# A recurrent block with a mixture of experts: first-layer outputs turned and halved by the pair

## The chip, the cores and the metric

One core of a Trainium2 chip runs one launch. The metric is the device time of the launch in microseconds (us).

## What is computed

The input has 4 sequences of 512 tokens with 256 features. It is normalised, and two branches are added to it. The first is a gated linear recurrence with a gated feed-forward layer of 1024 hidden features. The second is a mixture of 8 experts of which each token uses two:

```python
router_logits = x_flat @ w_router
top_vals, top_idx = jax.lax.top_k(router_logits, TOP_K)
probs = jax.nn.softmax(top_vals, axis=-1)
...
h = jnp.einsum('nc,ecd->ned', x_flat, w_fc)
h = jnp.square(jax.nn.relu(h))
y = jnp.einsum('ned,edc->nec', h, w_proj)
out = jnp.einsum('nec,ne->nc', y, w_tok)
...
x = x + _L0_attn_ref(xn, ...) + _L0_ffn_ref(xn, ...)
```

## The kernel before

Products of full precision are made of three products of halves: a tensor is split into a high part (a copy by ScalarE, ACT) and a low part (a subtraction by VectorE, DVE), and TensorE (PE) adds high by high, low by high and high by low.

After the routing, the tokens lie in DRAM sorted by expert, in 39 blocks of 128 rows (`NB`), each of one expert; two neighbouring blocks are a pair (`NP` = 20). A block runs through these helpers, whose names are the same on several engines:

- `load_pair` (SyncE's queue, SP) loads a pair into `xq`; `block_turn` (DVE) transposes it in 32 x 32 squares, `block_in` (ACT, then DVE) makes its halves, by the pair.
- `expert_in` (PE) is the first layer of one block. `block_relu` (ACT) and `block_square` (DVE) work by the pair, `store_act` (ACT's queue) stores the pair to DRAM in two DMAs, and `load_act` (SP) loads it back in four, in another order of rows, into a buffer `aq`. Only the loads wait for the store (`act_stored`), and the next turn of it waits for the loads (`aq_loaded`).
- `act_turn` (DVE, L1389) transposes one block from `aq` into `aT_raw`, `block_middle` makes `aT_hi` (ACT, L959) and `aT_lo` (DVE, L1396). There are two buffers `aT`, used in turn by blocks.
- `expert_out` (PE) is the second layer of a block, into one of two banks. `block_y` (ACT, L969) takes the result with its weight into `yb`, and `scatter` (GpSimd) writes it to DRAM.

The feed-forward layer runs beside this. Its 32 tiles are counted by d. `gate_up(d)` (PE), `gate` (ACT), `up` (DVE), `split_gu` (ACT and DVE) and `down(d)` (PE) follow each other; `take_down` (DVE) adds a finished sequence. Each engine has an order written out by hand. From d = 11 (`FIRST`) to 23 (`LAST`) a tile has two or three block steps; in step i PE does `expert_out(i - 8)` and `expert_in(i)`, parts of `gate_up` and `down` lie between, and DVE begins with `act_turn(i - 7)`. In some tiles a third step holds the output projection (`PROJECT`) or the turning (`TURN`) of a sequence of the first branch. At d = 24 and 25 (`DRAIN`) the last eight blocks' second layers run among the tiles. Only then are the outputs of the experts loaded and added (`add_sum`).

PE waits in `expert_out(i)` for the block's low half (`a_split`) and for `block_y(i - 2)` (`y_ready`). ACT's order at d = 24 is:

```python
split_gu(d - 1); block_relu(NP - 1); block_y(d0 - 1); block_middle(d0 + 1)
store_act(NP - 2); store_act(NP - 1)
block_y(d1 - 1); block_middle(d1 + 1); gate(d)
block_y(d2 - 1); block_middle(d2 + 1); block_y(d3 - 1); block_middle(d3 + 1)
```

Here d0 to d3 are blocks 31 to 34. All buffers lie in one arena at addresses given by hand, and some lie over others that are dead by then.

Of the kernel before, what the change touches and what calls it, by code (L numbers as in the profile page):

```python
# [14 lines left out]
P = 128  # L15
# [21 lines left out]
def recurrent_moe_block(nc, x, pre_norm_w, w_a, w_i, w_v, out_proj_w, decay_bias, ffn_norm_w,  # L37
# [35 lines left out]
    with ExitStack() as ctx:  # L73
# [27 lines left out]
        ident, ones = put("ident", [P, P]), put("ones", [P, P])  # L101
        before, ones_bf = put("before", [P, P], BF16), put("ones_bf", [P, P], BF16)
        one = put("one", [P, 1])
        half, minus_half, minus_one = put("half", [P, T]), put("minus_half", [P, T]), put("minus_one", [P, T])
        lane = put("lane", [P, P])
# [5 lines left out]
        HE = 2 * E  # L111
        Wr_wide = put("Wr_wide", [P, K, (2 * B - 1) * HE], F32R)
        Wr_at = (B - 1) * HE
        stats, mv = put("stats", [P, T, 6]), put("mv", [P, T, 2])
# [4 lines left out]
        of_slot = put("of_slot", [P, 2 * NP, 2])  # L119
# [101 lines left out]
        h2 = [h2_first] + [put(f"h2_{b}", [P, J, D], F32, cum_at if b != 2 else yb_at) for b in range(1, B)]  # L221
        junk = [junk_first] + [put(f"junk{b}", [P, J, D], BF16, cum_at if b != 2 else yb_at) for b in range(1, B)]
# [158 lines left out]
        def _(sp):  # L381
# [75 lines left out]
        def _(pe):  # L457
# [276 lines left out]
            def expert_out(i):  # L734

                if i >= 0:
                    if i == 0:
# [58 lines left out]
        def _(act):  # L796
# [156 lines left out]
            def block_middle(i):  # L953

                if 0 <= i < NB:
                    act.wait_ge(a_turned, i + 1)
                    if i >= 2:
                        act.wait_ge(pj_done, i - 1)
                    A.activation(aT[i % 2][0][:, :, :], aT[i % 2][2][:, :, :], ACT.Copy).then_inc(a_hi, 1)  # L959
# [101 lines left out]
            for d in range(FIRST, B * M):  # L1061
                if d <= LAST:
                    for v, i in enumerate(blocks_of(d)):
# [15 lines left out]
                elif d <= DRAIN:  # L1079
# [30 lines left out]
                if d in PROJECT or d in TURN:  # L1110
                    i = block_after(d)
                    block_y(i - LAG - 1)
                    block_middle(i - LAG + 1)
# [7 lines left out]
                    if d in TURN:  # L1121
                        split_h2(TURN[d], range(1, 2))

        @block.vector
        def _(dve):
# [148 lines left out]
            def experts():  # L1274
                be = [P, NB + 1, E]
                chain.step(V.tensor_tensor(past[:, :, :], blk_end[:, None, :].to_broadcast(be),
                                           lane[:, 0:NB + 1, None].to_broadcast(be), ALU.is_le))
# [103 lines left out]
            def act_turn(i):  # L1381

                if 0 <= i < NB:
                    n, v = divmod(i, 2)
                    u = act_home(n)
                    dve.wait_ge(aq_loaded[u], 16 * (P // Q) * (n // 2 + 1 if u < 2 else 1))
                    if i >= 2:
                        dve.wait_ge(pj_done, i - 1)
                    V.transpose(aT[i % 2][2][:, :, :].rearrange("p k (g s) -> p k g s", s=Q),  # L1389
                                aq[u][:, :, v, :, :]).then_inc(a_turned, 1)  # L1390

            def block_middle(i):

                if 0 <= i < NB:
# [343 lines left out]
```

## Time and profile before

| what | us |
|---|---|
| median of 3 runs | 271.26 (270.78 to 271.38) |
| the profiled execution's own time | 270.97 |
| its span | 269.2 |
| PE busy | 258.8 |
| DVE busy | 213.2 |
| ACT busy | 160.3 |

Times in the rows count from the start of the span. Busy times of PE are modelled from pipelined matmuls, so a busy PE is not PE at its peak. An engine's idle time is put down to what ended it.

### The profile page before, as it was taken

The page shows a single profiled execution, that of the slowest core. Times are in us where ns is not written, and L with a number is a line of the kernel's source. Part 1 is how long each engine was busy: PE and PEld are TensorE (multiplying, and loading weights), DVE is VectorE, ACT ScalarE, POOL GpSimd, SP SyncE. Part 2 cuts the span into 40 slices and gives each one's busy share as a digit, 9 for nine tenths or more (in the row PEclk, how much of TensorE's full clock was granted, in tenths as well). Part 3 has the DMA queues.
Part 4 walks back from the last instruction along what each step waited for, and adds up shares of the span by engine and source line. Part 5 has one row for each costly group of instructions (what it writes and reads, how often), then busy time and mean ns, then how long its engine had stood idle before and what let it go on. Part 6 is the DMA issues. An engine that isn't in the chain of part 4 may idle for free.

```text
span 269.2 us, 5120 instructions
## 1 busy us (share of the span) xinstructions
PE 258.8 (96%) x1593; PEld 227.2 (84%) x1593; DVE 213.2 (79%) x402; ACT 160.3 (60%) x323; POOL 117.1 (43%) x145
## 2 busy tenths in 40 slices
PE   5999999999999999999899999999999999999994
PEld 4767778888888888989798899989999999898883
DVE  4889999999846999699889895778778677732994
ACT  3888889995566554254764565466676665532221
POOL 6499004788878830016133244087336434550000
PEclk9999999999999999999999999999999999999999
DMA  6999962448621224639888777579979977529962
GB/s 198 354 391 323 322 187 99 158 169 254 234 98 49 92 83 93 48 79 181 154 201 191 181 186 172 128 150 223 211 157 235 202 181 176 136 76 299 385 237 78
DMA packets 107077, 49.62 MB, mean 184 GB/s; under 512 B 72006, under 2 KB 103756, under 8 KB 107052
## 3 DMA queue, kind: packets, MB, share of 16 engines
q1 hardware_dynamic: 90352, 32.48, 48.6%
q0 software_dynamic: 5664, 11.44, 14.6%
q10 hardware_dynamic: 11036, 5.38, 6.7%
q8 instruction: 14, 0.23, 0.3%
q14 instruction: 11, 0.09, 0.1%
HBM read 27.32 MB, written 21.96 MB: 183 GB/s over the span
## 4 chain that ended last, share of the span: by engine, by line
PE 69%; DVE 16%; issue 6%; ACT 4%; POOL 2%; DMA 1%; ACTq 0%; DVEq 0%; POOLq 0%
PE ps L459 62%; PE ps L547 5%; DVE rows_x L1331 2%; DVE xgT_raw L1363 2%; DVE act_e L1379 2%; DVE aT_raw L1389 1%; POOL rn L1597 1%; PE ps L560 1%; DMA rows_x<-in_L_attn_x_dram 1%; DVE stats L1134 1%; PE ps L476 1%; ACT aT_hi L959 1%; DVE hT_lo L1162 1%; DVE guT_lo L1301 1%; DVE cum L1188 1%
## 5 line engine op out<-in xcount | busy, mean ns | idle before, releaser
L1661 POOL DMA_INDIRECT y_dram<-yb,home_u x39 | 38.5, 988 | 59.6 <-ACT yb L969 57.2
L1638 POOL DMA_INDIRECT xs_dram<-rows_x,slot_u x32 | 38.6, 1205 | 11.3 <-issue 10.2
L459 PE MATMUL ps<-h2T_lo,Wgu_hi 128*128 128x512 f32 (+1 forms) x132 | 41.8, 386 | 0.0
L459 PE MATMUL ps<-h2T_hi,Wgu_hi 128*128 128x512 f32 (+1 forms) x132 | 41.0, 392 | 0.2 <-DVE rows_x L1202 0.2
L459 PE MATMUL ps<-h2T_hi,Wgu_lo 128*128 128x512 f32 (+1 forms) x132 | 40.4, 387 | 0.0
L459 PE MATMUL ps<-Wd_hi,guT_hi 128*128 128x256 f32 x128 | 36.5, 285 | 1.2 <-DVE guT_lo L1316 0.8
L959 ACT ACTIVATE aT_hi<-aT_raw 128x256 fp32r<-128x256 f32 x39 | 16.3, 417 | 33.9 <-DVE aT_raw L1389 33.8
L459 PE MATMUL ps<-Wd_hi,guT_lo 128*128 128x256 f32 x128 | 36.2, 282 | 0.0
L459 PE MATMUL ps<-Wd_lo,guT_hi 128*128 128x256 f32 x128 | 36.1, 282 | 0.0
L1296 DVE TENSOR_TENSOR gu<-gu,ps 128x512 f32<-128x512 f32 x31 | 21.1, 682 | 15.5 <-PE ps L459 15.3
L903 ACT ACTIVATE gu<-ps 128x512 f32<-128x512 f32 x31 | 18.5, 596 | 23.3 <-PE ps L459 21.7
L1396 DVE TENSOR_TENSOR aT_lo<-aT_raw,aT_hi 128x256 fp32r<-128x256 f32 x39 | 16.5, 424 | 16.7 <-ACT aT_hi L959 16.7
L923 ACT ACTIVATE guT_hi<-gu 128x512 fp32r<-128x512 f32 x31 | 19.4, 627 | 17.1 <-DVE gu L1296 13.9
L459 PEld LDWEIGHTS ps<-h2T_lo,Wgu_hi 128*128 128x128 f32 x132 | 24.5, 188 | 5.1
L459 PEld LDWEIGHTS ps<-h2T_hi,Wgu_lo 128*128 128x128 f32 x132 | 24.5, 188 | 4.8
L459 PEld LDWEIGHTS ps<-Wd_hi,guT_hi 128*128 128x128 f32 x128 | 24.1, 188 | 3.2 <-DVE guT_lo L1316 1.2
L459 PEld LDWEIGHTS ps<-Wd_lo,guT_hi 128*128 128x128 f32 x128 | 24.1, 189 | 1.2
L1301 DVE TENSOR_TENSOR guT_lo<-gu,guT_hi 128x512 fp32r<-128x512 f32 x31 | 20.9, 676 | 4.1 <-ACT guT_hi L923 3.8
L459 PEld LDWEIGHTS ps<-Wd_hi,guT_lo 128*128 128x128 f32 x128 | 24.1, 188 | 0.0
L459 PEld LDWEIGHTS ps<-h2T_hi,Wgu_hi 128*128 128x128 f32 x132 | 21.8, 188 | 2.2 <-DVE rows_x L1202 0.5
L969 ACT ACTIVATE yb<-ps,of_slot 128x256 f32<-128x256 f32 x39 | 18.4, 472 | 6.3 <-issue 3.5
L1613 POOL TENSOR_SCALAR sn<-ssq 128x4 f32<-128x4 f32 x4 | 0.8, 195 | 44.1 <-ACT junk L876 30.6
(174 smaller groups left out, 619.3 us busy)
## 6 DMA issues: line engine op xcount, KB each, us to landing
xs_dram<-blank SPq DMA_DIRECT2D x1, 5160.0 KB, 26.7
xq<-xs_dram SPq DMA_DIRECT2D x80, 64.0 KB
act_dram<-act_e ACTq DMA_DIRECT2D x40, 128.0 KB
aq<-act_dram SPq DMA_DIRECT2D x80, 64.0 KB, 2.4
sums<-y_dram SPq DMA_DIRECT2D x8, 512.0 KB, 7.8
Wgu_raw<-in_L_attn_w_gate_up_dram SPq DMA_DIRECT2D x4, 512.0 KB, 9.1
Wfc_raw<-in_L_ffn_w_fc_dram SPq DMA_DIRECT2D x16, 128.0 KB
Wpj_raw<-in_L_ffn_w_proj_dram SPq DMA_DIRECT2D x4, 512.0 KB, 6.5
```

Source lines behind the costliest of these rows:

```text
L459: return nc.tensor.matmul(dst, lhs, rhs, start=start, stop=stop, skip_group_check=group)
L547: last = nc.tensor.matmul(ps[:, aside(b) + side, (j % 2) * D:(j % 2 + 1) * D], dec[b][:, k, j * P:(j + 1) * P], Wo[:, k, :], start=k == 0, ...
L903: A.activation(gu[d % 2][:, :], ps[:, gu_bank(d), :], ACT.Silu).then_inc(sg_ready, 1)
L923: A.activation(guT[d % 2][0][:, :], gu[d % 2][:, :], ACT.Copy).then_inc(gu_hi, 1)
L959: A.activation(aT[i % 2][0][:, :, :], aT[i % 2][2][:, :, :], ACT.Copy).then_inc(a_hi, 1)
L969: A.activation(yb[i % YB][:, :], ps[:, PJ[i % 2], 0:D], ACT.Copy, scale=of_slot[:, i, 0:1]).then_inc(y_ready, 1)
L1296: V.tensor_tensor(gu[d % 2][:, :], gu[d % 2][:, :], ps[:, gu_bank(d) + 1, :], ALU.mult).then_inc(gu_ready, 1)
L1301: V.tensor_tensor(guT[d % 2][1][:, :], gu[d % 2][:, :], guT[d % 2][0][:, :].bitcast(F32), ALU.subtract).then_inc(gu_split, 1)
L1331: ins = V.tensor_tensor(Y[b][:, :, :], Y[b][:, :, :], sums[u][b][:, :, :], ALU.add)
L1396: V.tensor_tensor(aT[i % 2][1][:, :, :], aT[i % 2][2][:, :, :], aT[i % 2][0][:, :, :].bitcast(F32), ALU.subtract).then_inc(a_split, 1)
L1638: pool.indirect_dma_start(out=xs_dram, in_=rows_x[:, b, j, :], in_offset=None, out_offset=bass.IndirectOffsetOnAxis(ap=slot_u[:, n:n + 1], ...
L1661: pool.indirect_dma_start(out=y_dram, in_=yb[i % YB][:, :], in_offset=None, out_offset=bass.IndirectOffsetOnAxis(ap=home_u[:, i:i + 1], ax ...
```

## The change

The first layer's outputs are turned and halved by the pair: one transposition, one copy and one subtraction of 128 x 512 instead of two each of 128 x 256. The two `aT` buffers hold a pair each and so grow from 1 KB to 2 KB a half. The room for them is that of `yb`, which moves half to a place of its own and half over tables of the routing (`ones`, `before`, `ones_bf`, `Wr_wide`). `of_slot` moves over `stats`, the table `lane` is cut to the columns in use, and the buffer `h2` of sequence 2 comes to lie over the second `aT`; pair 1's turn waits until it has been read. Order and waits change with it: the pair's turn and its high half are at the even step i = 2n + 6 of pair n, the low half at the odd step after it, and the order in the drain is another.

```diff
+        early_at = room(0)
+        ones, before, ones_bf = put("ones", [P, P]), put("before", [P, P], BF16), put("ones_bf", [P, P], BF16)
+        HE = 2 * E
+        Wr_wide = put("Wr_wide", [P, K, (2 * B - 1) * HE], F32R)
+        lane = put("lane", [P, NB + 1])
...
-        aT = [turned_halves(f"aT{u}", 1) for u in range(2)]
-        yb_at = over[0]
-        yb = [small(f"yb{u}", [P, D]) for u in range(YB)]
+        h2_at = over[0] + 4 * KB
+        aT = [turned_halves(f"aT{u}", 2) for u in range(2)]
+        yb_at = room(2 * KB)
+        yb = [put(f"yb{u}", [P, D], F32, (yb_at, early_at)[u // 2] + D * 4 * (u % 2)) for u in range(YB)]
...
 (load_act, SP)
-                    sp.wait_ge(a_turned, 2 * n - 2)
+                    sp.wait_ge(a_turned, n - 1)
...
 (expert_out, PE)
-                    pe.wait_ge(a_split, i + 1)
+                    if v == 0:
+                        pe.wait_ge(a_split, n + 1)
                     if i >= 2:
                         pe.wait_ge(y_ready, i - 1)
-                    layer(PJ[i % 2], 0, aT[i % 2], slice(0, P), Wpj, expert[i], pj_done)
+                    layer(PJ[v], 0, aT[n % 2], slice(v * P, (v + 1) * P), Wpj, expert[i], pj_done)
...
 (ACT)
+            def block_middle(n):
+                if 0 <= n < NP:
+                    act.wait_ge(a_turned, n + 1)
+                    if n >= 2:
+                        act.wait_ge(pj_done, 2 * n - 2)
+                    A.activation(aT[n % 2][0][:, :, :], aT[n % 2][2][:, :, :], ACT.Copy).then_inc(a_hi, 1)
...
-                        block_middle(i - LAG + 1)
                         if i % 2 == 0:
+                            block_middle((i - LAG) // 2 + 1)
                             block_relu(i // 2 - 1)
...
                     if d == LAST + 1:
                         block_relu(NP - 1)
-                    block_y(d0 - 1)
-                    block_middle(d0 + 1)
-                    if d == LAST + 1:
+                        block_y(d0 - 1)
                         store_act(NP - 2)
                         store_act(NP - 1)
-                    block_y(d1 - 1)
-                    block_middle(d1 + 1)
+                        block_middle(NP - 3)
+                    else:
+                        block_middle(NP - 2)
+                        block_y(d0 - 1)
+                        block_middle(NP - 1)
                     gate(d)
-                    block_y(d2 - 1)
-                    block_middle(d2 + 1)
-                    block_y(d3 - 1)
-                    block_middle(d3 + 1)
+                    block_y(d0)
+                    block_y(d1)
+                    block_y(d2)
...
 (DVE)
+            def act_turn(n):
+                if 0 <= n < NP:
+                    u = act_home(n)
+                    dve.wait_ge(aq_loaded[u], 16 * (P // Q) * (n // 2 + 1 if u < 2 else 1))
+                    if n == 1:
+                        dve.wait_ge(h2T_done, K * 3)
+                    if n >= 2:
+                        dve.wait_ge(pj_done, 2 * n - 2)
+                    V.transpose(aT[n % 2][2][:, :, :].rearrange("p k (a s) -> p k a s", s=Q),
+                                aq[u][:, :, :, :, :].rearrange("p k v g c -> p k (v g) c")).then_inc(a_turned, 1)
...
-                        act_turn(i - LAG + 1)
+                        if i % 2 == 0:
+                            act_turn((i - LAG) // 2 + 1)
+                        else:
+                            block_middle((i - LAG + 1) // 2)
                         if v == 0 and d - 1 in PROJECT:
                             add_residual(PROJECT[d - 1], 1)
                         if v == 0:
                             split_gu(d - 1)
-                        block_middle(i - LAG + 1)
...
-                    d0, d1, d2, d3 = drained_by(d)
-                    act_turn(d0 + 1)
                     split_gu(d - 1)
                     if d == LAST + 1:
                         block_square(NP - 1)
-                    block_middle(d0 + 1)
-                    act_turn(d1 + 1)
-                    block_middle(d1 + 1)
-                    act_turn(d2 + 1)
-                    up(d)
-                    block_middle(d2 + 1)
-                    act_turn(d3 + 1)
-                    block_middle(d3 + 1)
+                        block_middle(NP - 4)
+                        act_turn(NP - 3)
+                        up(d)
+                        block_middle(NP - 3)
+                        act_turn(NP - 2)
+                    else:
+                        block_middle(NP - 2)
+                        act_turn(NP - 1)
+                        up(d)
+                        block_middle(NP - 1)
```

## Rows read from the trace of the kernel before

**Rows 1.** The page's engines: busy us (share of the span), instructions.

```profile
PE 258.8 (96%) x1593; PEld 227.2 (84%) x1593; DVE 213.2 (79%) x402; ACT 160.3 (60%) x323; POOL 117.1 (43%) x145
```

**Rows 2.** Three stretches: busy us of PE, weight loads, DVE, ACT, GpSimd; clock, DMA.

```profile
113.00:154.00 41.00, 39.52 (x258) 35.06 (x257) 36.46 (x66) 22.71 (x52) 11.95 (x13) 1.00 0.77 158
154.00:222.00 68.00, 67.83 (x475) 63.45 (x474) 51.37 (x103) 42.24 (x99) 31.74 (x33) 1.00 0.84 186
222.00:238.20 16.20, 16.09 (x108) 14.48 (x107) 10.63 (x23) 9.36 (x23) 7.74 (x8) 1.00 0.59 146
```

**Rows 3.** Groups by line and shape: busy us, mean ns | idle before, releaser.

```profile
L1389 DVE STREAM_TRANSPOSE aT_raw<-aq 128x256 f32<-128x256 f32 x39 | 16.9, 433 | 0.5 <-DMA aq<-act_dram 0.5
L459 PE MATMUL ps<-Wpj_hi,aT_hi 128*128 x78 | 16.7, 295 | 1.4 <-DVE aT_lo L1396 1.2
L1396 DVE TENSOR_TENSOR aT_lo<-aT_raw,aT_hi 128x256 fp32r<-128x256 f32 x39 | 16.5, 424 | 16.7 <-ACT aT_hi L959 16.7
L959 ACT ACTIVATE aT_hi<-aT_raw 128x256 fp32r<-128x256 f32 x39 | 16.3, 417 | 33.9 <-DVE aT_raw L1389 33.8
L1363 DVE STREAM_TRANSPOSE xgT_raw<-xq 128x512 f32<-128x512 f32 x20 | 14.1, 705 | 0.0
L1370 DVE TENSOR_TENSOR xgT_lo<-xgT_raw,xgT_hi 128x512 fp32r<-128x512 f32 x20 | 13.7, 687 | 0.9
L931 ACT ACTIVATE xgT_hi<-xgT_raw 128x512 fp32r<-128x512 f32 x20 | 12.4, 619 | 6.0 <-DVE xgT_raw L1363 6.0
```

**Rows 4.** Groups of the weight loads (PEld), 113 to 240 us.

```profile
L459 PEld LDWEIGHTS ps<-Wpj_hi,aT_hi 128*128 128x128 f32 x78 | 12.7, 188 | 4.4 <-issue 3.3
```

**Rows 5.** The last of the four loads of pair 0, by tile: issue, landing.

```profile
L404 SPq DMA_DIRECT2D aq<-act_dram x1: 488/488/488, 121.7 to 121.7; - x1
...
DMA to landing us min/median/max: 4.0/4.0/4.0
```

**Rows 6.** Timeline, 123 to 129 us: start, us, instruction, idle before and releaser.

```profile
124.06 0.67 DVE L1301 TENSOR_TENSOR guT_lo<-gu,guT_hi 128x512 fp32r<-128x512 f32 x1
...
125.67 0.28 PE L459 MATMUL ps<-Wd_hi,guT_hi 128*128 128x256 f32 x1
...
125.85 1.21 DVE L1291 TENSOR_TENSOR Wpj_lo<-Wpj_raw,Wpj_hi 128x1024 fp32r<-128x1024 f32 x1
...
128.56 0.48 PE L459 MATMUL ps<-Wpj_hi,aT_hi 128*128 x2 [0.57 <-DVE aT_lo L1396]
```

**Rows 7.** Timeline of the drain, 217 to 237 us.

```profile
218.04 0.43 ACTq L950 DMA_DIRECT2D act_dram<-act_e  x1
...
222.06 0.69 DVE L1379 TENSOR_TENSOR act_e<-ps,act_e 128x512 f32<-128x512 f32 x1
...
225.42 0.47 ACT L969 ACTIVATE yb<-ps,of_slot 128x256 f32<-128x256 f32 x1 [1.43 <-issue]
...
226.10 0.59 ACT L903 ACTIVATE gu<-ps 128x512 f32<-128x512 f32 x1
...
226.95 0.39 PE L459 MATMUL ps<-Wpj_hi,aT_hi 128*128 x2
...
227.15 0.45 DVE L1389 STREAM_TRANSPOSE aT_raw<-aq 128x256 f32<-128x256 f32 x1 [0.49 <-DMA aq<-act_dram]
...
229.69 1.28 DVE L1324 TENSOR_TENSOR rows_x<-rows_x,ps 128x512 f32<-128x512 f32 x2
...
230.89 0.44 DVE L1389 STREAM_TRANSPOSE aT_raw<-aq 128x256 f32<-128x256 f32 x1
...
232.37 0.47 PE L459 MATMUL ps<-Wpj_hi,aT_hi 128*128 x2
...
236.72 0.40 PE L459 MATMUL ps<-Wpj_hi,aT_hi 128*128 x2
```

**Rows 8.** The last of the four loads of pair 16, by tile.

```profile
L404 SPq DMA_DIRECT2D aq<-act_dram x1: 493/493/493, 218.6 to 218.6; - x1
...
DMA to landing us min/median/max: 3.5/3.5/3.5
```

More of the change, by code:

```diff
@@ L100, in recurrent_moe_block @@
         PRE_W, FFN_W, BIAS = 0, K, 2 * K
-        ident, ones = put("ident", [P, P]), put("ones", [P, P])
-        before, ones_bf = put("before", [P, P], BF16), put("ones_bf", [P, P], BF16)
+        ident = put("ident", [P, P])
+        early_at = room(0)
[3 more added lines that the diff above has]
+        lane = put("lane", [P, NB + 1])
+        assert top[0] - early_at >= 2 * KB
         one = put("one", [P, 1])
         half, minus_half, minus_one = put("half", [P, T]), put("minus_half", [P, T]), put("minus_one", [P, T])
-        lane = put("lane", [P, P])
         rank8 = put("rank8", [P, E])
@@ L108, in recurrent_moe_block @@
         Wr = put("Wr", [P, K, E])
-        HE = 2 * E
-        Wr_wide = put("Wr_wide", [P, K, (2 * B - 1) * HE], F32R)
         Wr_at = (B - 1) * HE
-        stats, mv = put("stats", [P, T, 6]), put("mv", [P, T, 2])
+        stats_at = room(4 * T * 6)
+        stats, mv = put("stats", [P, T, 6], F32, stats_at), put("mv", [P, T, 2])
         tv, rn1, nb1, negm = put("tv", [P, T]), put("rn1", [P, T]), put("nb1", [P, T]), put("negm", [P, T])
@@ L118, in recurrent_moe_block @@
         slot_u = put("slot_u", [P, TOP * T], U32)
-        of_slot = put("of_slot", [P, 2 * NP, 2])
+        of_slot = put("of_slot", [P, 2 * NP, 2], F32, stats_at)
         no_home, home_u = put("no_home", [P, 2 * NP]), put("home_u", [P, 2 * NP], U32)
@@ L219, in recurrent_moe_block @@
         act_e = [put(f"act_e{u}", [P, 2, D], F32, slot_at[2] + 4 * KB + 2 * D * 4 * u) for u in range(2)]
-        h2 = [h2_first] + [put(f"h2_{b}", [P, J, D], F32, cum_at if b != 2 else yb_at) for b in range(1, B)]
-        junk = [junk_first] + [put(f"junk{b}", [P, J, D], BF16, cum_at if b != 2 else yb_at) for b in range(1, B)]
+        h2 = [h2_first] + [put(f"h2_{b}", [P, J, D], F32, cum_at if b != 2 else h2_at) for b in range(1, B)]
+        junk = [junk_first] + [put(f"junk{b}", [P, J, D], BF16, cum_at if b != 2 else h2_at) for b in range(1, B)]
         ps = ctx.enter_context(nc.psum_tensor("ps", [P, 8, 512], F32))
@@ L736, in expert_out @@
                 if i >= 0:
+                    n, v = divmod(i, 2)
                     if i == 0:
@@ L1122, in _ @@
                         split_h2(TURN[d], range(1, 2))
+                    if i % 2 == 0:
+                        block_middle((i - LAG) // 2 + 1)
         @block.vector
@@ L1276, in experts @@
                 chain.step(V.tensor_tensor(past[:, :, :], blk_end[:, None, :].to_broadcast(be),
-                                           lane[:, 0:NB + 1, None].to_broadcast(be), ALU.is_le))
+                                           lane[:, :, None].to_broadcast(be), ALU.is_le))
                 chain.step(V.tensor_reduce(expert_f[:, :], past[:, :, :], AX.X, ALU.add))
@@ L1379, in block_square, with block_middle @@
                     V.tensor_tensor(mine, ps[:, FC[n % 2], 0:size], mine, ALU.mult).then_inc(act_ready, 1)
-            def act_turn(i):
-                if 0 <= i < NB:
-                    n, v = divmod(i, 2)
+            def act_turn(n):
+                if 0 <= n < NP:
                     u = act_home(n)
                     dve.wait_ge(aq_loaded[u], 16 * (P // Q) * (n // 2 + 1 if u < 2 else 1))
[L1387 to L1394, printed above, removed]
-                    dve.wait_ge(a_hi, i + 1)
-                    V.tensor_tensor(aT[i % 2][1][:, :, :], aT[i % 2][2][:, :, :], aT[i % 2][0][:, :, :].bitcast(F32),
+                    if n == 1:
[4 more added lines that the diff above has]
+                                aq[u][:, :, :, :, :].rearrange("p k v g c -> p k (v g) c")).then_inc(a_turned, 1)
+            def block_middle(n):
+                if 0 <= n < NP:
+                    dve.wait_ge(a_hi, n + 1)
+                    V.tensor_tensor(aT[n % 2][1][:, :, :], aT[n % 2][2][:, :, :], aT[n % 2][0][:, :, :].bitcast(F32),
                                     ALU.subtract).then_inc(a_split, 1)
@@ L1555, in _ @@
                     i = block_after(d)
-                    act_turn(i - LAG + 1)
-                    block_middle(i - LAG + 1)
+                    if i % 2 == 1:
+                        block_middle((i - LAG + 1) // 2)
+                    elif TURN.get(d) != 2:
+                        act_turn((i - LAG) // 2 + 1)
                     if d in PROJECT:
@@ L1570, in _ @@
                         split_h2(TURN[d], range(1, 2))
+                    if TURN.get(d) == 2:
+                        act_turn((i - LAG) // 2 + 1)
             add_down(B - 1)
@@ L1668, in tables @@
                 G.iota(rank8[:, :], pattern=[[-1, E]], base=E, channel_multiplier=0, **I)
-                G.iota(lane[:, :], pattern=[[1, P]], base=0, channel_multiplier=0, **I).then_inc(tables_ready, 1)
+                G.iota(lane[:, :], pattern=[[1, NB + 1]], base=0, channel_multiplier=0, **I).then_inc(tables_ready, 1)
             root_x(1, slice(0, 2))
```

8 lines of the change are left out of this document (1 added, 7 removed).

## The prediction

> **What bounds the kernel now.** I read the page's engine rows first: TensorE (PE) is busy 96% of the span [rows 1]. By stage, between 154 and 222 us PE has 67.83 of 68 us busy and its clock is granted in full in all three stages [rows 2]. So a faster VectorE (DVE) or ScalarE (ACT) gives time back only where PE waited for it. What is touched here is the way of the first layer's outputs into the second layer: turn on DVE, high half on ACT, low half on DVE. The groups by line show that this way stalls those two engines a lot (33.8 us of ACT before `aT_hi`, 16.7 us of DVE before `aT_lo`) and PE very little: 1.2 us before the second layer's first product [rows 3]. Idle time of the weight loads ahead of the same product is the upper view of that: 4.4 us, of which 3.3 without a releaser [rows 4].
>
> Last I read the timeline at the two ends of the block stage, where the order of the engines changes: around the first second-layer product (128.56 us) and in the drain, d = 24 and 25 [rows 6, 7]. The reader is to see there how close a load of `aq` lands to its use.
>
> **The change part by part.**
>
> *Fewer, larger instructions.* 39 turns of 433 ns become 20 of 705; 39 subtractions of 424 become 20 of 687; 39 ACT copies of 417 become 20 of 619 [rows 3]. DVE gives back 16.9 + 16.5 - 20 x (0.705 + 0.687) = 5.6 us, ACT 16.3 - 12.4 = 3.9 us. The round trip DVE, ACT, DVE inside one step also goes, since the low half is now made a step after the turn: the 16.7 us of DVE waits mostly vanish. On PE the worth is what PE waited: at least 1.2 us, at most 3.3 [rows 3, 4]. The first of these waits, 0.57 us at 128.56, stays, because the product there also needs `Wpj_lo`, whose 1.21 us run at 125.85 just ahead [rows 6]. That leaves 0.6 to 2.7; I take the middle, **-1.6 us**.
>
> The Trainium skill bears on this in "VectorE: DVE Perf Modes", section "The TRN2 errata — SBUF-src ops pay a fixed extra latency per instruction": many small tiles pay a fixed cost each, so tiles of 512 elements or more are advised. The rows agree on the size: 705 ns against twice 433 [rows 3]. "Perfetto Trace Analysis", section "Optimizing Scalar/DVE Operations", adds the condition that grouping helps "if the engine is saturated", and DVE at 51.37 of 68 us is not [rows 2]; by the first rule alone the result would be the gain of the first rival below, by the second none.
>
> *Moves of buffers.* `yb`, `stats`/`of_slot` and the tables change places only, and no instruction is added; the one new wait of the reuse (`h2T_done` before pair 1's turn) is at a place where the turn already stands behind the split of h2. `lane` shrinks in one GpSimd instruction that nothing on this path waits for late in the kernel. I cost all of it at nothing, within 0.1 us either way.
>
> *The turn comes a step earlier.* A pair is stored after its square in step 2n+2, and its turn stood at the head of steps 2n+7 and 2n+8; now one turn stands at the head of step 2n+6. Behind it on DVE are `split_gu` or `up`, `block_turn` and `block_square` of the same step; behind the copy it feeds on ACT are `block_relu` and `gate`. So a load that lands late now stops both engines.
>
> At the start: pair 0's last load is issued at 121.7 us and lands 4.0 us later, at 125.7 [rows 5]. DVE starts `guT_lo` at 124.06 and PE uses it at 125.67 [rows 6]. After the change the turn comes first: 125.7 + 0.71 + 0.67 = 127.1, so PE waits 1.4 us. Then `block_turn` 0.71, square 0.65, `Wpj_lo` 1.21 and the pair's subtraction 0.69 give 130.4 for the first second-layer product, against 128.56: **+1.8 us** [rows 3, 6]; the square is taken as that of the drain lasts, 0.69 less its overlap [rows 7]. Were the load early, the same sum from 124.06 is 128.7: +0.1. From here on the -1.6 works back, so PE should come to d = 24 between 1 us early and 1 us late.
>
> *The drain.* This decides. At d = 24 ACT now does the copy of pair 17 first, then `gate(24)`, and only then `block_y(31)`; PE's block 33 waits for that `y`. Before, `y` of block 31 ran at 225.42, ahead of all this. Pair 17's turn waited for its load until 227.15, the one turn of the kernel that did [rows 3, 7]. After: 227.15 + turn 0.71 + copy 0.62 + gate 0.59 + y 0.47, less small overlaps (`gate` starts before its forerunner's end), is 229.45; PE did block 33 at 226.95 [rows 3, 7]. So **+2.5 us** whatever came before, since it hangs on a load and not on PE.
>
> Pair 18 then: its square ended at 222.75. Now it comes after ACT's copy of pair 16, whose last load is issued at 218.6 and lands 3.5 us later, at 222.1 [rows 7, 8]: 222.1 + 0.71 + 0.62 + a relu of about 0.6 (taken as gate's 0.59) + hand-overs of 0.2 = 224.2, then the square: +2.1 us. Its turn, which stood at 230.89 without a wait, can come as late as 233.0. After it on DVE: the two `take_down` 1.28, `split_gu` 0.68, the subtraction 0.69: 233.0 + 0.71 + 2.65 = 236.3 at the latest. PE did block 36 at 232.37; with the +2.5 it wants 234.9. Its delay there is +2.5 to +3.9; I take the middle, **+3.2**, which also stays for block 38 (236.72 becomes 239.9) [rows 7]. Everything later (scatter, `sums`, last tiles) hangs on PE or on the last `y` and shifts along.
>
> **Sum.** The drain's +3.2 takes the place of what PE brought along (start +1.8, work -1.6, together +0.2), it isn't added to it: 270.97 + 3.2 = 274.2 us. The profiled execution lies 0.29 below the median of the runs, 271.26, so the forecast for a median is 274.2 to 274.5; I give **274.2**.
>
> Bounds of the drain. Below: with their waits gone DVE and ACT could run each earlier square about 1 us sooner (16.7 us of DVE waits over 39 blocks is 0.9 for two), so that pair 17 lands at 226: +1.4 there, +1.6 at the end, 272.6. Above: store to landing took 227.15 - 218.04 = 9.1 us [rows 7]; with turn, `split_gu`, `block_turn` and square behind it (2.75 us) a loop of four blocks takes 11.85 us, and PE's own pace from block 0 to block 33 is (226.95 - 128.56) / 33 = 2.98, 11.9 for four. There is no reserve, so slow loads add up; with 2 us more it is 276.5.
>
> **The rivals.**
>
> *Faster.* The loads come in time: squares, freed of the round trips, are stored so early that no turn waits, and only the removed PE waits are seen: 270.97 - 1.6 = 269.4. For it: 50 us of idle time on the two engines goes. It decides if pair 17 lands by about 224, 3 us sooner than now, or at 9.1 us from its store, if its square ends by 215. Against it: the store goes out at 218.04 now [rows 7], and the square will also stand behind pair 15's turn. Chance 0.17. This is also what the errata rule above would lead one to expect.
>
> *The same.* Pair 17 lands near 225 and the drain costs 1 to 2 us, against which the -1.6 can stand, if the start costs nothing; 271.0. Chance 0.11.
>
> *The loop becomes the bound.* Where four blocks take 12.75 us instead of 11.9 (a store to landing of 10 us), five rounds or so of the loop lose 0.85 us each, beside the drain: 274.2 + 4 = 278. For it: the first load's 4.0 us and pair 16's 3.5 us after issue [rows 5, 8]. Against it: the steps with the output projections give PE extra work and DVE room. Chance 0.10.
>
> **How the numbers follow.** The forecast has 0.62 and its own range is 272.6 to 276.5. Slower holds 0.62 + 0.10 = 0.72; 0.2% (0.54 us) is about what a measurement of this kernel can tell from no change, and 0.11 falls within it. The range leaves out most of the faster case at the low end and the loop at the high end: 270.2 to 277.0.
>
> **What would show it.** Right: 20 turns of about 0.70 us with DVE idle before several of them, released by the DMA of `aq`; a PE wait of over 1 us before a `Wd` product near 126 us; in the drain PE waits of 2 us or more before second-layer products, with ACT's `yb` behind `gu` and `aT_hi`; `aT_lo` no longer waiting for ACT. The granted clock is full in all rows of before [rows 2]; a drop during the drain's waits would be dearer than I reckon, and no row here prices it. Wrong: turns without DMA waits, or block 33 at or before 227 us.

## The result, and the profile after

The changed kernel took 276.65 us in the median of its first four runs (273.84 to 278.15) against 271.32 for the kernel before beside it: 1.0153 times, interval 1.0112 to 1.0194. Runs that count as slow are in the medians but not in the ratios: 278.15 here, one of drain_order's and one of after_slow's below. Four more executions (after_again below) gave 274.48 (272.50 to 275.75) against 271.54: 1.0107, interval 1.0045 to 1.0168. It is slower by 1 to 1.5%, and its times are spread over more than those of before.

The profiled execution took 273.84 us (span 272.1), 2.87 more than before's. These are the page's engines and three stretches, in the order of [rows 1, 2]:

```profile
PE 258.3 (95%) x1593; PEld 227.2 (83%) x1593; DVE 210.1 (77%) x364; ACT 156.8 (58%) x304; POOL 119.8 (44%) x145
```

```profile
113.00:154.00 41.00, 38.88 (x258) 35.06 (x258) 35.98 (x57) 22.50 (x49) 13.65 (x14) 1.00 0.81 163
154.00:222.00 68.00, 66.44 (x464) 61.89 (x464) 48.79 (x79) 38.88 (x83) 31.95 (x33) 1.00 0.84 180
222.00:238.20 16.20, 14.55 (x97) 12.72 (x96) 9.03 (x15) 7.95 (x17) 5.95 (x6) 1.00 0.57 132
```

TensorE idles 2.12, 1.56 and 1.65 us in the three stretches, where it idled 1.48, 0.17 and 0.11 [rows 2]: 3.6 us more, against the 2.87 that the time grew by. Some four fifths of that lie in the second and third stretch. The groups by line say what it waits for:

```profile
L465 PE MATMUL ps<-Wpj_hi,aT_hi 128*128 x78 | 16.6, 294 | 5.1 <-DVE aT_lo L1406 5.1
...
L1399 DVE STREAM_TRANSPOSE aT_raw<-aq 128x512 f32<-128x512 f32 x20 | 14.1, 707 | 11.3 <-DMA aq<-act_dram 11.2
...
L1406 DVE TENSOR_TENSOR aT_lo<-aT_raw,aT_hi 128x512 fp32r<-128x512 f32 x20 | 13.7, 686 | 0.7 <-ACT aT_hi L967 0.7
...
L967 ACT ACTIVATE aT_hi<-aT_raw 128x512 fp32r<-128x512 f32 x20 | 12.6, 631 | 31.2 <-DVE aT_raw L1399 31.2
```

Beside [rows 3]: turns and low halves cost 5.6 us less and the high halves 3.7 less, and the round trip on VectorE is gone (16.7 us of waits became 0.7). In its place the turn waits 11.2 us for loads of `aq`, where it waited 0.5; and TensorE waits 5.1 us for low halves, where it waited 1.2. The chain that ended last, in order of time (start, length, what ran), shows why the loads are late:

```profile
177.93 4.75 DMA act_dram<-act_e
...
184.25 3.20 DMA aq<-act_dram
187.48 0.72 DVE aT_raw L1399
...
188.76 0.58 ACT act_e L950
...
190.55 3.26 DMA act_dram<-act_e
...
202.65 3.24 DMA act_dram<-act_e
...
208.38 3.70 DMA aq<-act_dram
212.10 0.72 DVE aT_raw L1399
...
215.12 2.44 DMA act_dram<-act_e
...
219.12 4.00 DMA aq<-act_dram
223.15 0.72 DVE aT_raw L1399
...
226.16 2.01 DMA act_dram<-act_e
```

The chain runs from a pair's store through its load to its turn, and then, because the relu and square of the pair two later stand behind that turn and its copy, to the store of that later pair, and round again. Its stores (pairs 10, 12, 14, 16 and 18) follow each other by 12.62, 12.10, 12.47 and 11.04 us; TensorE's own pace is 11.9 for the same four blocks. TensorE doesn't stall on each round: it feels the lateness when it has added up. In all of 154 to 222 us it waits once, before block 28, the first of pair 14:

```profile
215.45 0.48 PE L465 MATMUL ps<-Wpj_hi,aT_hi 128*128 x2 [1.56 <-DVE aT_lo L1406]
```

Now the drain, beside [rows 7]:

```profile
223.15 0.71 DVE L1399 STREAM_TRANSPOSE aT_raw<-aq 128x512 f32<-128x512 f32 x1 [1.15 <-DMA aq<-act_dram]
...
227.39 0.55 PE L465 MATMUL ps<-Wpj_hi,aT_hi 128*128 x2 [1.12 <-DVE aT_lo L1406]
...
228.93 0.83 ACT L977 ACTIVATE yb<-ps,of_slot 128x256 f32<-128x256 f32 x2
...
229.63 0.39 PE L465 MATMUL ps<-Wpj_hi,aT_hi 128*128 x2
...
235.28 0.48 PE L465 MATMUL ps<-Wpj_hi,aT_hi 128*128 x2 [0.53 <-DVE aT_lo L1406]
...
239.62 0.40 PE L465 MATMUL ps<-Wpj_hi,aT_hi 128*128 x2
```

Block 33 starts at 229.63 (226.95 before), block 36 at 235.28 (232.37), block 38 at 239.62 (236.72): 2.7 to 2.9 us late. Here block 33 itself waits for nothing; block 32 before it was late, since pair 16's turn waited for its load until 223.15. Block 31 had started 1.27 us late (224.00, before 222.73); the other 1.63 us are lost from there to block 38.

### The profile page after: what moved, and what is told of

Its sections match the earlier page's. It is cut to its first block, busy times and chain, and to the rows that moved or that the text cites. A ratio compares the mean times of both kernels' runs of the same rounds, so it can differ in the third digit from the quotient of the medians.

```text
span 272.1 us, 5007 instructions
## 1 busy us (share of the span) xinstructions
PE 258.3 (95%) x1593; PEld 227.2 (83%) x1593; DVE 210.1 (77%) x364; ACT 156.8 (58%) x304; POOL 119.8 (44%) x145
## 4 chain that ended last, share of the span: by engine, by line
PE 44%; DMA 19%; DVE 14%; issue 7%; ACT 6%; SPq 5%; POOL 3%; ACTq 1%; POOLq 0%; DVEq 0%
PE ps L465 36%; DMA aq<-act_dram 7%; DMA act_dram<-act_e 7%; PE ps L553 5%; SPq L410 4%; DMA sums<-y_dram 3%; DVE aT_raw L1399 2%; SPq L452 2%; DVE rows_x L1340 2%; PE ps L469 1%; ACT act_e L950 1%; PE ps L482 1%; DVE guT_lo L1310 1%; POOL y_dram L1677 1%; DVE xgT_raw L1372 1%
## 5 line engine op out<-in xcount | busy, mean ns | idle before, releaser
L1677 POOL DMA_INDIRECT y_dram<-yb,home_u x39 | 41.0, 1051 | 61.1 <-ACT yb L977 57.8
L967 ACT ACTIVATE aT_hi<-aT_raw 128x512 fp32r<-128x512 f32 x20 | 12.6, 631 | 31.2 <-DVE aT_raw L1399 31.2
L1399 DVE STREAM_TRANSPOSE aT_raw<-aq 128x512 f32<-128x512 f32 x20 | 14.1, 707 | 11.3 <-DMA aq<-act_dram 11.2
L465 PE MATMUL ps<-Wpj_hi,aT_hi 128*128 x78 | 16.6, 294 | 5.1 <-DVE aT_lo L1406 5.1
```

The lines of the kernel that those rows point to most:

```text
L465: return nc.tensor.matmul(dst, lhs, rhs, start=start, stop=stop, skip_group_check=group)
L967: A.activation(aT[n % 2][0][:, :, :], aT[n % 2][2][:, :, :], ACT.Copy).then_inc(a_hi, 1)
L1399: V.transpose(aT[n % 2][2][:, :, :].rearrange("p k (a s) -> p k a s", s=Q), aq[u][:, :, :, :, :].rearrange("p k v g c -> p k (v g) c")).th ...
L1677: pool.indirect_dma_start(out=y_dram, in_=yb[i % YB][:, :], in_offset=None, out_offset=bass.IndirectOffsetOnAxis(ap=home_u[:, i:i + 1], ax ...
```

## The experiments

**after_again.** The changed kernel itself, for its spread and a second profile.

> The changed kernel itself, for the spread of its times and a second profile. Theory L: its time hangs on when loads land, above all pair 0's at the start: 274 to 277.5, and in a profiled run slower than the first one's 273.8 the first turn has waited for its load, or the waits before blocks 28 to 36 are longer. Rival (its first profile shows all that it loses): within 0.5 us of 273.8 each time.

274.48 us, 272.50 to 275.75: not the same loss each time. Of the executions of 276 us and more none has a profile. The second profile (274.74 us) loses nothing at the start and nothing before the drain (block 28 at 213.06, 1.1 us earlier than before's 214.19), and then all at once:

```profile
227.45 0.71 DVE L1399 STREAM_TRANSPOSE aT_raw<-aq 128x512 f32<-128x512 f32 x1 [2.63 <-DMA aq<-act_dram]
...
228.20 0.63 ACT L967 ACTIVATE aT_hi<-aT_raw 128x512 fp32r<-128x512 f32 x1 [4.47 <-DVE aT_raw L1399]
228.73 0.58 ACT L911 ACTIVATE gu<-ps 128x512 f32<-128x512 f32 x1
229.21 0.83 ACT L977 ACTIVATE yb<-ps,of_slot 128x256 f32<-128x256 f32 x2
...
229.81 0.77 PE L465 MATMUL ps<-Wpj_hi,aT_hi 128*128 x2 [2.52 <-ACT yb L977]
...
231.22 0.41 PE L465 MATMUL ps<-Wd_hi,guT_hi 128*128 128x256 f32 x1
...
233.31 0.40 PE L465 MATMUL ps<-Wpj_hi,aT_hi 128*128 x2
```

This is the forecast's drain instruction by instruction: turn of pair 17, copy, `gate(24)`, `y` of block 31, block 33. The granted clock then adds to it. The three products of block 33 and the down products behind it take 3.50 us (229.81 to 233.31) where the first profile has 2.13 for the same work (229.63 to 231.76); a `Wd` product has 0.41 us, not 0.28. The chain of this profile has the loop too, but its stores of pairs 13, 15 and 17 (195.69, 207.54, 219.43) follow each other by 11.85 and 11.89 us, TensorE's own pace, and TensorE waits for none of them ahead of the drain. The windows of this profile:

```profile
222.00:238.20 16.20, 12.73 (x72) 10.85 (x70) 8.09 (x13) 7.04 (x17) 5.21 (x5) 0.89 0.56 131
...
230.00:233.00 3.00, 3.00 (x16) 3.00 (x17) 1.39 (x3) 1.56 (x4) 2.39 (x3) 0.55 0.62 140
```

**drain_order.** In the drain, `y` of block 31 and the gate go ahead of the copies on ScalarE.

```diff
                         store_act(NP - 1)
+                        block_y(d0)
+                        gate(d)
                         block_middle(NP - 3)
                     else:
                         block_middle(NP - 2)
                         block_y(d0 - 1)
+                        block_y(d0)
+                        gate(d)
                         block_middle(NP - 1)
-                    gate(d)
-                    block_y(d0)
                     block_y(d1)
```

> The changed kernel, with only ACT's order in the drain altered: block_y(31) and gate(24) ahead of the copy of pair 17, block_y(35) and gate(25) ahead of the copy of pair 19. Theory D: PE's waits in the drain fall by about 2.5 us, 271 to 273. Theory L: pair 16 and pair 18 are late because their loads are, and the order of ACT changes less than 0.7 us: 273 to 277, as the changed kernel.

275.49 us, 1.0106 times before (1.0072 to 1.0140): no gain over the changed kernel that can be told. In its profile block 33 doesn't wait for `y`, but block 32 and block 36 wait 0.81 and 1.10 us for low halves. Taking the `y` out of the way of the late load does not make the load early. This profile also shows the start as the forecast had it:

```profile
126.55 0.71 DVE L1401 STREAM_TRANSPOSE aT_raw<-aq 128x512 f32<-128x512 f32 x1 [1.77 <-DMA aq<-act_dram]
127.19 0.65 DVE L1312 TENSOR_TENSOR guT_lo<-gu,guT_hi 128x512 fp32r<-128x512 f32 x1
...
127.89 0.39 PE L465 MATMUL ps<-Wd_hi,guT_hi 128*128 128x256 f32 x1 [1.44 <-DVE guT_lo L1312]
```

**stale_load.** Pair *n* is loaded from what was stored for pair *n* - 2, so no load waits for its own store. All pairs but the first two get another pair's data; everything else is issued as in the changed kernel.

```diff
-                sp.wait_ge(act_stored[n % 2], 32 * (n // 2 + 1))
+                sp.wait_ge(act_stored[n % 2], 32 * (max(n - 2, n % 2) // 2 + 1))
+                of = max(n - 2, n % 2)
...
-                                 act_pair[n, :, :, r * Q:(r + 1) * Q]).then_inc(aq_loaded[u], 16)
+                                 act_pair[of, :, :, r * Q:(r + 1) * Q]).then_inc(aq_loaded[u], 16)
```

> The changed kernel, but pair n is loaded from the stored data of pair n - 2 (pairs 0 and 1 from their own) and waits for that store alone, so the second layer works on other rows than the reference's. Number and size of the transfers are the same. Theory L: no turn waits for a load of its own loop any more, PE's waits before the second layer nearly vanish, 268.5 to 270.5. Theory D: the copy of pair 17 still stands ahead of block_y(31), but its load is early, so it also falls, to 270 to 271.5; the two differ little here. If the waits come from contention among the transfers, not from the store: no change, 273 to 277.

272.12 us, 1.0004 times before (0.9974 to 1.0034): the loss is gone, though the time lies above the ranges of both theories. From 154 us to the end of the drain TensorE never idles:

```profile
154.00:222.00 68.00, 68.00 (x478) 63.75 (x478) 49.57 (x81) 39.91 (x85) 33.30 (x33) 1.00 0.89 191
222.00:238.20 16.20, 16.20 (x109) 14.34 (x109) 9.84 (x16) 9.11 (x20) 8.11 (x8) 1.00 0.38 107
```

This profile too has the late start, as pairs 0 and 1 still wait for their own stores: pair 0's turn waited 1.17 us and block 0 came at 130.19, 1.63 late. Block 38 came at 236.75, against 236.72 [rows 7]: without late loads the new form gains 1.6 us between the two.

**stale_end.** The same for pairs 14 to 19 alone.

```diff
+                of = n if n < 14 else n - 2
+                sp.wait_ge(act_stored[n % 2], 32 * (of // 2 + 1))
```

> The changed kernel with only its last six pairs, 14 to 19, loaded from what was stored for the pair two before them; their second-layer outputs are those of other blocks, all earlier pairs wait for their own store as in the changed kernel. Theory D2 (the forecast's sum: the price falls due from pair 14 on, and takes the place of what was lost and won before): 271 to 271.8, the same as before within 0.2%. Theory L2 (start and loop cost their time all through the stage, and nothing of it is caught up): 272.5 to 274, with the changed kernel at 274.5 to 276.6 and the kernel whose loads are stale from pair 2 on at 272.1.

274.53 us against 272.45: 1.0070 times (1.0045 to 1.0096). With the last six pairs on time about half of the loss (0.70% of 1.07 to 1.53) is still there. In its profile the drain costs nothing (block 31 to block 38 takes 13.97 us, before 13.99), and the loss lies earlier: block 0 came 1.71 us late, and pair 4's turn waited 3.47 us for its load, TensorE 2.96 us for its low half, and the clock fell behind that.

```profile
157.44 0.77 PE L466 MATMUL ps<-Wpj_hi,aT_hi 128*128 x2 [2.96 <-DVE aT_lo L1407]
```

```profile
158.50:160.00 1.50, 1.50 (x6) 1.31 (x6) 0.63 (x2) 0.84 (x2) 0.00 (x0) 0.50 0.57 133
```

**late_turn.** In every even step the turn stands behind the gathered pair's turn and the square, and the copy behind relu and gate.

```diff
-                        if i % 2 == 0:
-                            act_turn((i - LAG) // 2 + 1)
-                        else:
+                        if i % 2 == 1:
                             block_middle((i - LAG + 1) // 2)
...
                             block_square(i // 2 - 1)
+                            act_turn((i - LAG) // 2 + 1)
```

> The changed kernel, with the pair's turn moved behind block_turn and block_square of the same even step, and ACT's copy behind block_relu and gate; the drain is left as changed. Theory L (a loop: store, load, turn, then the square and store of the pair two later, which stand behind that turn, 11.9 to 12.6 us for four blocks): the loop is cut, the turns' DMA waits shrink to under 3 us in all, PE's wait before block 28 (1.7 us in the changed kernel's trace) goes, and the time falls to 269.5 to 271.5. Theory D (a fixed price of the drain's order, +2.5 to +3.2, as forecast): the drain stays, 273 to 275.

277.50 us, 1.0195 times (1.0158 to 1.0231): no better than the changed kernel, by the medians worse. The loop is cut (the turns wait 1.7 us for loads in all, not 11.2), but the low half, a step later, now comes late mostly without any DMA's doing: TensorE waits 5.1 us for low halves and `y`, as much as before the cut. For `h` (normalised rows that ScalarE writes and TensorE transposes) it waits 2.8 us, but 1.48 of them at 84.65 us, ahead of the block stage, as in moves_only below. Behind the first of these waits the clock falls: 0.72 granted between 132 and 138 us.

**start_fix, start_fix_stale.** Pair 0's turn stands at the end of its step, as block 0's did before; the second kernel has the stale loads too, with the same part of the output from other data.

```diff
-                        if i % 2 == 0:
+                        if i % 2 == 0 and i != LAG - 2:
                             act_turn((i - LAG) // 2 + 1)
...
                             weights_lo(16)
+                            act_turn(0)
```

> The changed kernel with one order altered: pair 0's turn on VectorE, and ScalarE's copy of it, stand at the end of step 6 (behind the split of expert hidden part 12, the turn and square of the pair of that step and the weights' low half) in place of its start, as block 0's turn did before the change. Theory L (two separate prices: some 1.8 us at the start because the split stands behind a wait for pair 0's load, and some 3 us late in the stage because store, load, turn and square form a loop longer than TensorE's four blocks): the start's price goes, the loop's stays, median 273.5 to 274.8, and the waits before blocks 28, 32 and 36 of the second layer remain in the profile. Theory E (only the early lateness counts, the later waits are its echo): 270.5 to 271.5. Theory N (what is lost at the start is caught up by the end, so the loop alone sets the time): unchanged from the changed kernel, 275.5 to 277.

> The same as start_fix, and each pair from 2 on is loaded from what was stored for the pair two before it, so that its load no longer waits for its own store; the output of the second layer is that of other blocks for all pairs but the first two. It prices the larger instructions with no late load anywhere. Theory L: with both prices gone the gain of the removed waits is left, 269.3 to 270.6 (the kernel with the stale load alone was at 272.1 and had 1.85 us of lateness at the start). Theory N (early lateness is caught up): 271.7 to 272.5, as the stale load alone.

start_fix: 275.23 us, 1.0139 times (1.0088 to 1.0190); within its spread no better. No `Wd` product waits at the start, but the turn and its copy now stand behind the weights' split, and block 0 comes at 129.32 after a wait of 1.28 us: a larger turn finds no free place there either. In its drain block 33 waits for `y` as the forecast had it:

```profile
231.09 0.48 PE L465 MATMUL ps<-Wpj_hi,aT_hi 128*128 x2 [1.66 <-ACT yb L977]
```

start_fix_stale: 270.51 us, 0.9978 times (0.9955 to 1.0001), so with every load but the first two pairs' early the larger instructions are worth some 0.8 us, which the interval hardly tells from nothing. Its ten runs fall in two groups, seven at 270.32 to 270.61 with a mean clock of 1.000 and three at 271.82 to 272.12 with 0.994. The profiled one is of the second group, and this is its place, behind the wait of 1.28 us for block 0 and one for `h`:

```profile
133.00:134.00 1.00, 1.00 (x7) 1.00 (x7) 1.00 (x2) 0.25 (x1) 0.00 (x0) 0.50 0.77 127
```

**square_first.** start_fix, and in every even step VectorE squares ahead of the turn, ScalarE's relu ahead of its copy.

```diff
+                        if i % 2 == 0:
+                            block_square(i // 2 - 1)
+                            if i != LAG - 2:
+                                act_turn((i - LAG) // 2 + 1)
                         if v == 1:
                             up(d)
                         if i % 2 == 0:
                             block_turn(i // 2 + 1)
-                            block_square(i // 2 - 1)
```

> start_fix with the loop cut in another way: in each even step VectorE squares the pair of the step before it turns the pair whose load may be late (ScalarE's relu ahead of its copy likewise), so that a late load no longer delays the next store; the turn stays ahead of the up product and of the gathered pair's turn, so that its low half is not late as it was when the turn stood behind all of them. Theory L: the wait of a turn no longer feeds the next pair's store, 270 to 272, at most one or two waits of TensorE before second-layer products. Rival (any late turn is paid by TensorE, whatever stands behind it, because its buffer pair and LAG give no slack): 274 to 276 as start_fix or more, with as many waits before second-layer products as there.

276.01 us, 1.0143 times (1.0092 to 1.0195). In the middle it did what was wanted: the turns wait 2.6 us for loads in all, and no second-layer product waits more than 0.2 us between 136 and 228 us. But block 0 waits 2.12 us, a stretch at the lower clock follows (0.50 granted from 134 to 136 us), and blocks 32 and 33 wait 0.71 and 1.05.

**best.** From step 8 on the order of square_first, before that the changed kernel's; the second layer's weight split ahead of pair 0's turn; the drain as in drain_order.

```diff
+                        if i % 2 == 0:
+                            if i >= LAG:
+                                block_square(i // 2 - 1)
+                            if i == LAG - 2:
+                                weights_lo(16)
+                            act_turn((i - LAG) // 2 + 1)
...
                             block_turn(i // 2 + 1)
-                            block_square(i // 2 - 1)
+                            if i < LAG:
+                                block_square(i // 2 - 1)
```

> The changed kernel with three orders altered. From step 8 on VectorE squares ahead of the turn, and the turn stands behind the split of the expert hidden part and ahead of the up product; before that the square keeps its place, and the second layer's weight split stands ahead of pair 0's turn, where VectorE waited for that pair's load; ScalarE's relu stands ahead of its copy, and in the drain y ahead of the gate and the copies. Theory L (start and loop are the whole price): start and middle without waits, at most 1 to 1.5 us left in the drain, 269.8 to 271.5. Rival (any late turn is paid somewhere): 273 to 275.

273.46 us, 1.0074 times (1.0043 to 1.0106): by the ratios a third to a half of the loss is back, but the intervals overlap with the changed kernel's, so this gain isn't clear of the scatter. It is less than expected, and it doesn't beat the kernel before. TensorE's waits for low halves are 2.3 us (5.1 in the changed kernel), but waits for `h` have grown from 0.4 to 1.8.

**after_slow, before_slow.** Two loads of 8 bytes a partition ahead of each pair's four, in the changed kernel and in the one before.

```diff
+                for r in range(2):
+                    mine = slice(64 * r, 64 * r + 64)
+                    sp.dma_start(spare[mine, 2 * n:2 * n + 2], x_t[0][mine, 0, 2 * n:2 * n + 2]).then_inc(spare_loaded, 16)
                 for r in range(P // Q):
```

> The changed kernel with two small loads of 8 bytes a partition issued ahead of each pair's four loads, some 1 us more of issue by the spacing of the loads there (1.5 us for four). Theory L: the loop of four blocks is longer by 1 us at each of its turns, so late loads begin sooner and cost more, 279 to 284. Theory E (only the start's lateness counts): 277 to 278, by the 1 us that pair 0's load is later. Rival (the loads' queue has slack and the end does not hang on it): 276 to 277, unchanged.

> The kernel before with the same two small loads of 8 bytes a partition ahead of each pair's four loads that cost the changed kernel some 18 us (some 1 to 1.5 us later landing of each pair). Theory L (the change took the reserve between a load's landing and its turn, and closed the loop): before has that reserve, so 271.3 to 272.5, at most one wait more in the drain. Rival (the extra loads themselves cost the time, whatever waits for them): 280 or more.

after_slow: 289.54 us, 1.0710 times before (1.0634 to 1.0787); before_slow: 276.39, 1.0216 (1.0165 to 1.0268). The groups of turn and product, first of after_slow, then of before_slow:

```profile
L471 PE MATMUL ps<-Wpj_hi,aT_hi 128*128 x78 | 16.9, 297 | 8.2 <-DVE aT_lo L1412 5.8 <-ACT yb L983 2.4
...
L1405 DVE STREAM_TRANSPOSE aT_raw<-aq 128x512 f32<-128x512 f32 x20 | 14.2, 710 | 30.3 <-DMA aq<-act_dram 30.3
```

```profile
L1395 DVE STREAM_TRANSPOSE aT_raw<-aq 128x256 f32<-128x256 f32 x39 | 17.0, 435 | 7.8 <-DMA aq<-act_dram 7.6
...
L465 PE MATMUL ps<-Wpj_hi,aT_hi 128*128 x78 | 16.8, 297 | 5.4 <-DVE aT_lo L1402 5.3
```

Both were dearer than expected. The same two loads cost the changed kernel 13 to 15 us and the old one 5. after_slow's chain runs through stores, loads and turns for most of the block stage, as the loop says. In the old one another thing shows, which my expectation left out: SyncE, which also issues the loads of the gathered pairs, had hardly any room for two more. From 154 to 222 us its issues take 62.4 of 68 us in before_slow (47.1 before, 42.5 in the changed kernel), and before_slow's chain is almost nothing but such issues, gathered pairs (L378), small loads (L408) and `aq` (L410), from 185 to 219 us:

```profile
185.16 0.60 SPq L408
185.80 0.59 SPq L410
...
218.26 0.59 SPq L410
218.89 2.73 DMA aq<-act_dram
```

So before_slow doesn't say how large the old form's reserve was, and a part of after_slow's price can be issuing too (58.0 of 68 us). With 7.6 us of turn waits and 15.65 us from block 31 to block 38 it looks much like the changed kernel with its own loads.

**moves_only.** The kernel before with the moves of buffers alone.

```diff
-        yb_at = over[0]
-        yb = [small(f"yb{u}", [P, D]) for u in range(YB)]
...
+        yb_at = room(2 * KB)
+        yb = [put(f"yb{u}", [P, D], F32, (yb_at, early_at)[u // 2] + D * 4 * (u % 2)) for u in range(YB)]
```

> The kernel before, with only the moves of buffers: yb half over the routing's tables and half at a place of its own, of_slot over stats, lane cut to 40 columns, h2 of sequence 2 where yb was. Both theories: no difference, 271.3 within 0.5. If the places of the buffers cost something: 272 or more.

272.54 us, 1.0028 times (1.0009 to 1.0047): 0.2 to 1.3 us above before, small but clear of the interval, and as the rival in my expectation had it (272 or more). In its profile the block stage is that of before, shifted by some 1 us; the shift is one wait of TensorE for `h`:

```profile
84.58 1.09 PE L564 MATMUL ps<-ident,h 128*128 128x128 f32 x8 [1.48 <-ACT h L886]
```

It is 0.4 us in both profiles of the changed kernel, which moves the same buffers, and 1.48 again in late_turn's and square_first's. So it comes and goes among kernels with the moves; neither profile of a kernel without them has it. Whether it is a price of the moves or scatter these runs don't settle. From block 31 to block 38 moves_only takes 13.99 us, as before.

## Why the prediction was right, and where it wasn't

**The forecast.** 274.2 us, slower, with a range of 270.2 to 277.0: the medians of 276.65 and 274.48 lie in it, the first just above the forecast's own range of 272.6 to 276.5. The sign, the kind of wait and the place of most terms hold. The way in which they were added doesn't; the clock was left unpriced and the moves were put at nothing. That the second median lies within 0.3 us of the forecast is therefore in part luck.

**Fewer, larger instructions, -1.6.** Right. The durations came as read from the rows of the gathered pairs, VectorE's waits for the copy went, and with stale loads TensorE gained 1.6 us between block 0 and block 38 in the one profile. As a kernel the gain is some 0.8 us (start_fix_stale).

**Moves of buffers, nothing within 0.1 us.** Not borne out: moves_only took 0.2 to 1.3 us more than before. It is a part of the loss at most, as stale_load and start_fix_stale have the same moves and no loss.

**The start, +1.8.** Right in size: block 0 came 1.63 us late in stale_load's profile, 1.71 in stale_end's and 2.56 in drain_order's (where VectorE was 0.65 us late before the turn). But it isn't always there. In two profiles of the changed kernel the load had landed when VectorE came to the turn at 124.0 and block 0 was on time; in three others with the same order the turn waited 1.2 to 1.8 us. That can be a part of the wider spread.

**The drain, +3.2.** The size was right: block 38 came 2.9 and 3.8 us late in the two profiles, inside the +2.5 to +3.9. The mechanism written down for it, `y` of block 31 behind copy and gate, was shown whole in one of the two (229.81 against a reckoned 229.45), with pair 17's load at 227.45 against 227.15; start_fix's profile has it too (1.66 us). In the other profile pair 16's late load had delayed block 32 already. Seen from block 31 to block 38, which takes 13.99 us before, the drain costs 1.63 and 4.82 us in the changed kernel's two profiles (the second with the lower clock), 1.06 to 2.09 with the other orders, and nothing where its loads are stale (13.75 to 13.97 us in stale_load, stale_end and start_fix_stale). So the drain has a price of its own, and it is that of the loads. The step that fails is "+2.5 us whatever came before": the `y` is where a late load shows, not what makes it cost. With the `y` ahead the time stayed (drain_order), and the drain still cost 1.92 us.

**The sum.** "The drain's +3.2 takes the place of what PE brought along, it isn't added to it" is the step that failed. With the last six pairs on time, the sum leaves 0.2 us above before (271.2); 2.1 us were measured (274.53 against 272.45). Late loads cost time at pairs from 0 on, in other places in each profile, and in stale_end's, where the drain cost nothing, what was lost early stayed lost. Only where every load from pair 2 on is early (stale_load) is the loss gone, which shows late loads as its cause.

**The loop.** It had a chance of 0.10 and a price of 4 us beside the drain. The forecast took it for unlikely, and both profiles' chains show it: closed over four rounds of 11.0 to 12.6 us against TensorE's 11.9 in the first, at 11.9 in the second, and two small loads more ahead of each pair cost 13 to 15 us (after_slow), though a part of these can be SyncE's issuing. From store to turn the first chain takes 8.0 to 9.6 us, where the forecast's 9.1 gave a loop of 11.85: the reckoning without reserve was right, its chance too low. That the way round, and not the late loads alone, makes the loss is argued from the chains: in the profiles of late_turn and square_first, which cut it, the turns wait 1.7 and 2.6 us for loads, but other waits came in, and neither is faster. What spoke against it in the forecast, room in the steps with output projections, may be why after_again is 1.1 us ahead at block 28; it doesn't last. The trips themselves are 2.4 to 4.8 us for a store's part of the loop and 3.2 to 4.0 for the last load's, beside 1.5 us and more in which SyncE issues four loads. The Trainium skill, in "DMA: Bandwidth & Descriptors", section "Anatomy of one DMA — SWDGE (gpsimd) path", fits some 2.0 us plus bytes by 436 GB/s to a DMA that GpSimd issues. Carried over to these DMAs, which ScalarE and SyncE issue, it gives an estimate of 2.3 us for the 128 KB store and 2.15 for a 64 KB load, which would leave the loop some 2 us of reserve. The section doesn't claim this for such DMAs, the chain shows longer trips, and the chain decides.

**The clock.** The forecast named it as unpriced. Behind waits of TensorE the granted clock falls to its lower level, 1.2 of 2.4 GHz (0.50 in the rows of start_fix_stale and stale_end), for some 3 us, and that costs 1.4 us more (after_again, 3.50 against 2.13 us) or 1.5 (the two groups of start_fix_stale). The Trainium skill, in "TensorE: Matmul & The Clock Gate", section "What's actually happening", has the same two levels, the lower one for an array that has idled; these rows agree. But it doesn't explain the spread of the changed kernel: 276.47 has a mean clock of 0.999 and 275.75 one of 1.000, while 276.84 has 0.992 and 274.74 has 0.994.

**What stays open.** The loss can't be given as one split over start, middle and drain, since each execution has its own: at block 31 the changed kernel is 1.27 us late in its first profile and 0.99 early in its second. What lost more in its executions of 276 us and above isn't shown. Why the same load lands 1 to 2 us later in one execution than in another was not tried. No order tried brings the larger instructions and early loads together; best is 0.7% slower than before.

## What to carry to other kernels

An order that moves a consumer of a DMA to an earlier place should be read as a loop: what stands behind the waiting instruction on its engine, and does that lead to the next store of the same stream? Where the loop's length is about the pace of the bounding engine, the larger and fewer instructions that the consumer gained count for little; price the loop first, with the slowest landing in the trace and not the median. An order that cuts the loop must still bring the consumer's result in time: two that did so here were no faster. And don't let a late wait "take the place" of an early one in the sum, unless something in the trace shows that the early loss is caught up.

## What was not expected of the hardware

Two tiny loads ahead of four on the same queue (8 bytes a partition) made the kernel 13 to 15 us slower by the medians, and the one before 5; there SyncE's issuing had become the chain, at 0.45 to 0.6 us for most single issues. And the same waits at the start, 1.28 us for block 0 and some 0.25 for `h` just behind, were followed by the lower clock in start_fix_stale's profile (mean 0.994) and not in start_fix's (mean 1.000).
